# Two fused convolution layers in a software pipeline: folded value weights, three convolution banks, halved transfers and orders written out over all images

## The reference

```python
def _forward(x, gate_w, gate_b, value_w, geom_w, geom_b, pw_w, pw_b):
    gate = einsum('bchw,rc->brhw', x, gate_w) + gate_b ; mu = softmax(gate over r)      # R = 4
    v = einsum('bchw,dc->bdhw', x, value_w)                                             # 1x1, 32 -> 32
    patches = the nine 3x3 neighbours of v, zero padded
    g = einsum('bchw,gc->bghw', x, geom_w) + geom_b   # theta, base, hyper for each r
    ...
    kern = exp(-(pu / sig_u) ** 2 - (ps / sig_s) ** 2)          # nine weights per pixel and r
    w = mu * kern ; w = w / (sum of w over r and the nine + 1e-06)
    agg = einsum('brsl,bcsl->brcl', w, patches)                 # 4 * 32 channels
    return einsum('bkhw,ok->bohw', agg, pw_w) + pw_b            # 128 -> 32
x = x + _forward(gn(x), ...)
x = x + conv3x3(conv3x3(conv3x3(gn(x), w1), w2), w3)            # 32 -> 64 -> 64 -> 32
```

## Time and profile before

| | us |
|---|---|
| median of three runs | 549.23 |
| the profiled execution, its own time | 549.03 |
| its span, first to last instruction | 547.2 |
| outside the span | 1.83 |
| TensorE busy (modelled) | 483.3 |
| VectorE busy | 419.4 |
| ScalarE busy | 216.3 |
| GpSimd busy | 191.4 |

### The profile page before, as it was taken

The page is one execution under the profiler, slowest core; times in us unless marked ns, Lnnn a source line. Parts: engine busy times, 40 slices in busy tenths (PEclk is TensorE's granted clock), DMA queues, the critical chain, the costliest instruction groups (busy, mean ns, idle before and its releaser), DMA issues.

```text
span 547.2 us, 7160 instructions
## 1 busy us (share of the span) xinstructions
PE 483.3 (88%) x2527; PEld 391.8 (72%) x2527; DVE 419.4 (77%) x553; ACT 216.3 (40%) x408; POOL 191.4 (35%) x95
## 2 busy tenths in 40 slices
PE   2505973789999999999999999999999999998995
PEld 2204752566887788777977797779777987886894
DVE  2598678999898989898989989998989698412211
ACT  1520631265335543643355344644364313340110
...
GB/s 145 42 1 0 5 0 56 98 72 17 46 97 100 40 38 87 93 59 44 69 95 69 47 53 107 65 55 41 100 77 25 36 95 86 22 56 107 70 5 38
DMA packets 40275, 32.23 MB, mean 59 GB/s; under 512 B 26160, under 2 KB 30768, under 8 KB 40240
## 3 DMA queue, kind: packets, MB, share of 16 engines
...
## 4 chain that ended last, share of the span: by engine, by line
PE 64%; DVE 16%; issue 9%; SPq 4%; ACT 2%; POOL 1%; DMA 1%; DVEq 0%; ACTq 0%; POOLq 0%
PE conv_ps L366 42%; PE agg_ps L427 7%; DVE prod L712 6%; DVE prod L722 5%; PE val_ps L412 5%; SPq L287 4%; PE geo_ps L395 3%; PE geo_ps L386 3%; PE pw_ps L440 2%; PE conv_ps L380 2%; DMA xraw<-in_x 1%; POOL prod L1003 1%; DVE st L546 1%; DVE trig L643 1%; POOL vs L1019 1%
## 5 line engine op out<-in xcount | busy, mean ns | idle before, releaser
L712 DVE TENSOR_TENSOR prod<-val_ps,tapw 128x2048 f32<-128x2048 f32 x80 | 181.0, 2284 | 11.6 <-PE val_ps L412 10.2
L366 PE MATMUL conv_ps<-c_hi,wc_hi 128*128 128x448 f32 (+2 forms) x384 | 157.1, 409 | 0.0
L366 PE MATMUL conv_ps<-c_hi,wc_lo 128*128 128x448 f32 (+2 forms) x384 | 144.6, 376 | 0.0
L366 PE MATMUL conv_ps<-c_lo,wc_hi 128*128 128x448 f32 (+2 forms) x384 | 144.1, 375 | 0.0
L1003 POOL TENSOR_TENSOR prod<-prod 128x2048 f32<-128x2048 f32 x23 | 112.5, 4894 | 16.4 <-DVE prod L712 16.4
L1019 POOL TENSOR_TENSOR vs<-vn 128x1024 f32<-128x1024 f32 x32 | 69.6, 2185 | 74.2 <-ACT vn L843 73.4
L722 DVE TENSOR_TENSOR prod<-prod 128x2048 f32<-128x2048 f32 x35 | 88.7, 2533 | 1.0 <-POOL prod L1003 0.5
L366 PEld LDWEIGHTS conv_ps<-c_hi,wc_hi 128*128 128x128 f32 x384 | 72.5, 189 | 21.7 <-issue 8.3
L366 PEld LDWEIGHTS conv_ps<-c_hi,wc_lo 128*128 128x128 f32 x384 | 72.3, 188 | 10.6
L366 PEld LDWEIGHTS conv_ps<-c_lo,wc_hi 128*128 128x128 f32 x384 | 72.7, 189 | 9.7 <-issue 2.4
L929 ACT ACTIVATE c_hi<-conv_ps 128x512 fp32r<-128x512 f32 (+4 forms) x88 | 41.9, 485 | 86.4 <-PE conv_ps L366 86.2
...
## 6 DMA issues: line engine op xcount, KB each, us to landing
xq_hi<-y_hi SPq DMA_DIRECT2D x128, 66.0 KB, 2.0
xq_lo<-y_lo SPq DMA_DIRECT2D x128, 66.0 KB, 2.0
...
x2r<-x SPq DMA_DIRECT2D x128, 32.0 KB, 1.9
...
```

The costliest lines, as they stand in the source:

```text
L366: mm = nc.tensor.matmul(bank[:, 0:conv_cols(n)], weights, lo if part == 1 else hi, start=term == part == 0, stop=final and part == 2)
L712: v.tensor_tensor(dst, val.unsqueeze(2).to_broadcast([P, B, R, C]), wgt.unsqueeze(3).to_broadcast([P, B, R, C]), ALU.mult).then_inc(mult_d ...
```

## The change

1. The value matrix is no longer applied to the image. `fold` multiplies it into the pointwise matrix once (`out_w`), and the taps are taken on the normed image: `v_product` and `v_evict` are gone, `norm1_padded` writes the padded copy `xn`, and `xc` has two buffers.
2. `agg_ps` has one bank instead of two, `conv_ps` three instead of two.
3. The high and the low part of y and of xq stand in one tile each, and one DMA moves both: 16 relayout DMAs an image instead of 32. They all wait for the low part.
4. `body` and `on` are gone: each engine's order is a list over all images. In it `store`, `load_x` and `halo` stand elsewhere among the DMAs, and the convolution lags less and less behind the front.

```diff
+N_AGG, N_CONV = 1, 3
+        y = sb("y", [P, 2, 2, K8, PW])
+        y_hi, y_lo = y[:, 0].bitcast(F32R), y[:, 1]
+        xq = sb("xq", [P, 2, H // 2 + 2, PW], F32R)
+            def by_slots(i, g):
                 if g == 0:
+                    wait(y_lo_done, i + 1)
+                    if i >= 1:
+                        wait(conv_done, N_CHUNK * (i - 1) + 4)
                 for s in range(4):
                     j0 = (2, 1, 1, 0)[s] + K8 * g
+                    sp.dma_start(xq[C * s:C * s + C, :, j0:j0 + K8, :].bitcast(F32),
+                                 y[C * g:C * g + C, :, (s + 1) % 2, :, :]).then_inc(xq_in[g], 16)
...
+                    before = N_CHUNK * j + n - N_CONV
+                    if before >= 0:
+                        pj, pn = divmod(before, N_CHUNK)
+                        if pn < N_SPLIT:
+                            wait_lows(pe, pj, pn + 1)
+                        else:
+                            pe.wait_ge(out_done, 2 * pj + pn - N_SPLIT + 1)
...
+            def fold(i, n):
+                if i > 0:
+                    return
+                if n == 0:
+                    pe.wait_ge(front_consts_in, 16 * N_FRONT_CONSTS)
+                    pe.wait_ge(back_consts_in, 16 * N_BACK_CONSTS)
+                    nc.tensor.transpose(pw_ps[:, 0:P], val_w_sb[:, :], ident_sb[:, :]).then_inc(fold_pe, 1)
+                else:
+                    pe.wait_ge(fold_a, 1)
+                    nc.tensor.matmul(pw_ps[:, P:P + C], val_t[:, :], pw_t_sb[:, :], start=True,
+                                     stop=True).then_inc(fold_pe, 1)
...
-            def v_product(i, h):
-                if h == 0:
-                    pe.wait_ge(ch_v, CH_V * i + 1)
-                else:
-                    pe.wait_ge(vc_out, 2 * i + 1)
-                nc.tensor.matmul(geo_ps[:, :], val_w_sb[:, :], xc[:, h * BANK:(h + 1) * BANK],
-                                 start=True, stop=True).then_inc(v_mm, 1)
...
-                if n >= 2 or i >= 1:
-                    pe.wait_ge(agg_sb, 8 * i + n - 1)
+                if 8 * i + n >= N_AGG:
+                    pe.wait_ge(agg_sb, 8 * i + n + 1 - N_AGG)
...
+            def norm1_padded(i):
                 act.wait_ge(gn1_v, GN_V * i + 8)
                 if i >= 1:
                     act.wait_ge(pairs_done, 4 * i)
+                s.activation(xn[:, 1:1 + QR, 1:1 + W], xraw[:, i % 2, :].rearrange("p (r w) -> p r w", w=W),
+                             ACT.Identity, scale=gn1[:, 3:4], bias=gn1[:, 4:5]).then_inc(xp_done, 1)
```

TensorE's new order up to the first back transpose of image 2, and the end of it:

```diff
+gn1_sums(0, 0)
+gn1_sums(0, 1)
+geometry(0)
+gn1_sums(1, 0)
+values(0, 0)
+values(0, 1)
+gn1_sums(1, 1)
+values(0, 2)
+fold(0, 0)
+fold(0, 1)
+values(0, 3)
+values(0, 4)
+geometry(1)
+values(0, 5)
+transpose_sums(0, 0)
+values(0, 6)
+transpose_sums(0, 1)
+values(0, 7)
+transpose_sums(0, 2)
+transpose_sums(0, 3)
+values(0, 8)
+values(0, 9)
+pointwise(0, 0)
+transpose_sums(0, 4)
+values(1, 0)
+transpose_sums(0, 5)
+values(1, 1)
+transpose_sums(0, 6)
+values(1, 2)
+transpose_sums(0, 7)
+pointwise(0, 1)
+values(1, 3)
+values(1, 4)
+values(1, 5)
+gn2_sums(0, 0)
+values(1, 6)
+gn1_sums(2, 0)
+gn2_sums(0, 1)
+gn1_sums(2, 1)
+values(1, 7)
+transpose_sums(1, 0)
+geometry(2)
+transpose_sums(1, 1)
+values(1, 8)
+values(1, 9)
+transpose_sums(1, 2)
+transpose_sums(1, 3)
+convs(0, 0, 8)
+take_high(0, 0)
+convs(0, 8, 11)
+take_high(0, 1)
+take_high(0, 2)
+convs(0, 11, 12)
+pointwise(1, 0)
+values(2, 0)
+convs(0, 12, 14)
+values(2, 1)
+convs(0, 14, 17)
+transpose_sums(1, 4)
+convs(0, 17, 21)
+take_high(0, 3)
+transpose_sums(1, 5)
+take_high(0, 4)
+convs(0, 21, 23)
+transpose_sums(1, 6)
+convs(0, 23, 24)
+transpose_sums(1, 7)
+convs(0, 24, 26)
+values(2, 2)
+pointwise(1, 1)
+values(2, 3)
+convs(0, 26, 28)
+values(2, 4)
+convs(0, 28, 31)
+take_high(0, 5)
+convs(0, 31, 36)
+values(2, 5)
+values(2, 6)
+gn1_sums(3, 0)
+convs(0, 36, 37)
+take_high(0, 6)
+convs(0, 37, 39)
+gn2_sums(1, 0)
+gn1_sums(3, 1)
+take_high(0, 7)
+gn2_sums(1, 1)
+convs(0, 39, 42)
+transpose_sums(2, 0)
...
+convs(6, 29, 34)
+take_high(6, 5)
+convs(6, 34, 36)
+take_high(6, 6)
+convs(6, 36, 38)
+gn2_sums(7, 0)
+convs(6, 38, 40)
+take_high(6, 7)
+gn2_sums(7, 1)
+convs(6, 40, 49)
+take_high(6, 8)
+convs(6, 49, 60)
+convs(7, 0, 60)
```

VectorE's new order up to the products that this transpose needs:

```diff
+gn1_stats(0)
+gn1_spread(0)
+gn1_scale(0)
+gn1_bias(0)
+tap_weights(0, 0)
+tap_weights(0, 1)
+tap_weights(0, 2)
+tap_weights(0, 3)
+split_weights(0)
+tap_weights(0, 4)
+gn1_stats(1)
+tap_weights(0, 5)
+gn1_spread(1)
+tap_weights(0, 6)
+gn1_scale(1)
+tap_weights(0, 7)
+mult(0, 0)
+gn1_bias(1)
+mult(0, 1)
+mult(0, 2)
+mult(0, 3)
+mult(0, 4)
+tap_weights(1, 0)
+tap_weights(1, 1)
+mult(0, 5)
+tap_weights(1, 2)
+mult(0, 6)
+tap_weights(1, 3)
+mult(0, 7)
+mult(0, 8)
+tap_weights(1, 4)
+mult(0, 9)
+tap_weights(1, 5)
+residual(0, 0)
+tap_weights(1, 6)
+tap_weights(1, 7)
+mult(1, 0)
+mult(1, 1)
+mult(1, 2)
+gn2_stats(0, 0)
+residual(0, 1)
+gn2_stats(0, 1)
+mult(1, 3)
+mult(1, 4)
+gn1_stats(2)
+gn2_spread(0)
+gn1_spread(2)
+gn2_scale(0)
+gn1_scale(2)
+add_products(1, 0, 2)
+gn1_bias(2)
+gn2_bias(0)
+add_products(1, 0, 3)
+mult(1, 5)
+split_low(0)
+mult(1, 6)
+mult(1, 7)
+mult(1, 8)
+mult(1, 9)
+tap_weights(2, 0)
+tap_weights(2, 1)
+add_products(1, 1, 1)
+tap_weights(2, 2)
+tap_weights(2, 3)
+add_products(1, 1, 2)
+tap_weights(2, 4)
+add_products(1, 1, 3)
+tap_weights(2, 5)
+residual(1, 0)
+tap_weights(2, 6)
+tap_weights(2, 7)
+mult(2, 0)
+mult(2, 1)
+mult(2, 2)
+residual(1, 1)
+mult(2, 3)
+gn2_stats(1, 0)
+mult(2, 4)
+gn1_stats(3)
+gn2_stats(1, 1)
+gn1_spread(3)
+add_products(2, 0, 2)
+gn2_spread(1)
+gn1_scale(3)
+add_products(2, 0, 3)
...
```

ScalarE's:

```diff
+norm1_padded(0)
+norm1(0)
+split_weights(0)
+tap_weights(0, 0)
+tap_weights(0, 1)
+tap_weights(0, 2)
+tap_weights(0, 3)
+tap_weights(0, 4)
+tap_weights(0, 5)
+fold(0, 0)
+norm1(1)
+norm1_padded(1)
+tap_weights(1, 0)
+sums_out(0, 0)
+tap_weights(1, 1)
+sums_out(0, 1)
+tap_weights(1, 2)
+fold(0, 1)
+sums_out(0, 2)
+tap_weights(1, 3)
+sums_out(0, 3)
+tap_weights(1, 4)
+tap_weights(1, 5)
+sums_out(0, 4)
+sums_out(0, 5)
+sums_out(0, 6)
+sums_out(0, 7)
+norm1_padded(2)
+norm2(0)
+split_high(0)
+norm1(2)
+sums_out(1, 0)
+sums_out(1, 1)
+sums_out(1, 2)
+sums_out(1, 3)
+tap_weights(2, 0)
+high_part(0, 0)
+low_part(0, 0)
+high_part(0, 1)
+high_part(0, 2)
+tap_weights(2, 1)
+tap_weights(2, 2)
+low_part(0, 1)
+tap_weights(2, 3)
+tap_weights(2, 4)
+high_part(0, 3)
+low_part(0, 2)
+sums_out(1, 4)
+tap_weights(2, 5)
...
```

GpSimd's:

```diff
+gn1_rstd(0)
+pair_sum(0, 0)
+pair_sum(0, 1)
+gn1_rstd(1)
+pair_sum(0, 2)
+pair_sum(0, 3)
+add_products(0, 0, 0)
+pair_sum(1, 0)
+pair_sum(1, 1)
+add_products(0, 1, 0)
+pair_sum(1, 2)
+add_products(1, 0, 0)
+pair_sum(1, 3)
+add_products(1, 0, 1)
+gn2_rstd(0)
+gn1_rstd(2)
+pair_sum(2, 0)
+pair_sum(2, 1)
+add_products(1, 1, 0)
+pair_sum(2, 2)
+pair_sum(2, 3)
+add_products(2, 0, 0)
+add_products(2, 0, 1)
...
```

1177 lines of the change are left out of this document (928 added, 249 removed).

## The result

The changed kernel takes 541.7 us (median of 4 runs, 541.2 to 542.8), the kernel before in the same session 548.8: ratio 0.9874, 95% interval 0.9853 to 0.9894. Shorter, as forecast, and clear of the noise, but by 1.3% and not by 3.8%; a threshold of 2% would call it the same. 541.7 lies just outside the range of 516 to 541. The profiled execution took 541.5 us, its span 539.6.

What follows compares the result with a forecast made beforehand. VectorE's chain was taken to bound the fill and TensorE the steady part: 146.5 + 372.2 + 2.4 = 521.1 us for the last matmul, plus 5.9 and 1.83 outside the span, 528.8, stated as 528.5 us, range 516 to 541.

Steps and rivals of the forecast that it cites:

- The fill: Start of the run, by VectorE's list: image 2's first back transpose at 146.5 us, TensorE waiting for VectorE about 7 us.
- The tail: Last image's convolution: norm, splits and joint transfers take 12.5 us, covered by 14.2 us of TensorE work, 1.7 to spare.
- The removed work: Value products of five images behind the first convolution: 10 x 0.86 = 8.6 us off TensorE, the bound engine.
- the shorter walk: Rival, fill: VectorE's list is shorter than summed, TensorE reaches image 2's back transpose at 139; 520 us, chance 0.15.
- transfers by part: Rival, last image: a joint DMA costs as much as two, adding 9 us; 537 us, chance 0.05.
- the one bank at 0.6 us for each transpose: Rival, behind 146.5 us: single agg_ps bank stops each of 48 back transposes, 29 us in all; 556 us, chance 0.04.
- The lower clock: Rival, fill: TensorE runs at its lower clock, image 0's transposes take 3.5 us; 537 us, chance 0.16.
- the walk: VectorE's instructions in the fill, summed in list order to the adds image 2's first back transpose needs, 146.5 us.
- From there TensorE's sum: From image 2's first back transpose to the last matmul: TensorE's work, 372.2 us, plus 2.4 us of waiting.
- Transfers: 0 in the steady part: Joint DMAs save 9.9 us of SyncE per image, which waits anyway in the steady part: worth 0 there.
- the shared port: Fill: VectorE instructions with two SBUF inputs and GpSimd's take turns; the five adds could make it up to 10 us longer.
- priced them at 0 to 1 us in all: Banks: three convolution banks worth 0; one agg_ps bank costs 1 us in all, within the 2.4 us of waiting.

Runs made afterwards that it cites:

- prod_back: Changed kernel with the two value products put back on TensorE for images 3 to 7, their result unread: 549.6 us, 1.0007 of the kernel before.
- old_late: old_order with one more wait, GpSimd's first pair sum of an image held until VectorE's part 3 of its tap weights: 536.4 us, 0.9772 of the kernel before.
- slot3_first: Changed kernel with the same 16 relayout transfers reordered and counted so a first chunk needs five instead of eight: 538.3 us, 0.9799 of the kernel before.
- new_split: Changed kernel with high and low parts in separate transfers, 32 relayout transfers an image instead of 16: 600.5 us, 1.093 of the kernel before.
- recip_norm: Changed kernel with GpSimd's power for both norms replaced by a reciprocal on VectorE, computing other numbers: 542.6 us, 0.9894 of the kernel before.
- norm2_first: Changed kernel with norm2(i) and split_high(i) ahead of image i+2's first norms on ScalarE, images 2 to 5: 546.7 us, 0.9965 of the kernel before.
- pow_free: Changed kernel with a product moved ahead of a VectorE add during GpSimd's power, norm biases ahead of adds, five images: 562.0 us, 1.0222 of the kernel before.
- the four hybrids: Changed kernel's lists for the fill, then old_late's order, with different changeover points or banks: 541.9, 537.1, 546.1 and 553.8 us.
- hybrid4: hybrid3 with the changed kernel's banks, one for back transposes and three for the convolution: 553.8 us, 1.0084 of the kernel before.
- hybrid3: Changed kernel's lists up to image 2's first back transpose, then old_late's order, two banks each: 546.1 us, 0.9947 of the kernel before.
- old_order: All new operations and joint transfers in the kernel before's five repeating orders, two banks each: 552.8 us, 1.0059 of the kernel before.

## Why the prediction was wrong, by its own steps

**Right.** The fill: `mult(0, 0)` 32.05 (33.1 forecast), `mult(1, 0)` 70.53 (68.7), `mult(2, 0)` 127.65 (126), the back transpose of image 2 at 147.86 (146.5), with VectorE as what it waits for. The first convolution came at about 106, not at 102.5: some of the waiting that I had put behind it lay ahead of it. The tail: no stop, transfers at 0.64 us each. The removed work: 8.6 us by the rows, 7.9 by `prod_back` (8.6, less 2.1 of waits, plus 3.1 of clock, less 0.9 of a fill that came out shorter, each from its one profile). Of the rivals, the shorter walk, transfers by part and the one bank at 0.6 us for each transpose did not come. The lower clock did in part: PEclk was 0.50 from 60.2 to 67.0 us, where it had been 1.00, and image 0's fifth back transpose took 3.17 us; from 90 to 106 us it was 0.55 (0.50 before). With the 4.60 us of the tap-weight instruction, which the walk had at under 0.5, this is part of why `mult(1, 0)` came 1.8 us late although `mult(0, 0)` came 1.1 us early. All of it is inside the 1.4 us at the back transpose of image 2, so that term came out partly by errors that cancel.

**Wrong.** One step: "From there TensorE's sum", and in it the waiting, 2.4 us forecast and 13.6 measured. With 1.4 us from the fill that is the whole miss of 12.6 us in the span. The sentence that failed is "VectorE's 52.2 us an image are now less than TensorE's share ... so it runs ahead and its wait goes": I took waiting to be a matter of the share of each engine, and asked only for VectorE. Its adds cost TensorE 0.6 us in one image; xq cost 5.05, ScalarE's parts and VectorE's result 5.4. What made them late is the orders as a whole, since the same operations under the old orders wait little (`old_late`, below). That an image's norm, transfers and low parts now stand where their consumer comes first is my reading of the lists, shown for the transfers alone. What the runs say of it:

- xq: all 5.05 us of xq waits went when the first chunk waited for five transfers instead of eight (`slot3_first`), but only 3.4 us came back in the time, and the same edit is worth nothing in `old_late`. Waits for c_lo grew from 2.4 to 4.5 us, and behind one of them the granted clock was 0.50 from 403.2 to 406.6 us, which costs 1.6. "Transfers: 0 in the steady part" was the same mistake; `new_split` shows that this path has no slack there.
- It is no single instruction. The slow power (`recip_norm`), ScalarE's order (`norm2_first`) and VectorE's (`pow_free`) were each tried, and gained nothing or lost 5 to 20 us. Each list is written to fit the others. (The 1.5 us that `recip_norm` gained behind the fill bound what the power cost, as far as one profile tells.)
- It is not that TensorE cannot be kept full with this work. `old_late`, with all the new operations, waits about 1 us an image; its 55.2 us compare with 55.9 - 1.72 = 54.2 us of work by the earlier trace rows. It gives 536.4 although its convolution begins over 5 us later than the changed kernel's. The remainder to my 528.5 is mostly that start, by this estimate from the rows.

The forecast sum was thus a sum of two things that no kernel here has together, the new fill and a full steady part. Whether they can be had together stays open: the four hybrids lost at the seam what the fill had gained, for reasons of their own, and `hybrid4` lost more behind it. One bank against two was not tried alone in the changed kernel, whose orders need three banks for the convolution. The nearest is `hybrid4` against `hybrid3`: 57.5 us an image against 55.3 to 56.1, so the banks, with the places that they ask for, can cost up to 2 us an image. I had priced them at 0 to 1 us in all; what they cost in the changed kernel's own orders stays open.

**What I had seen and not used.** The prediction weighed the shared port ("SBUF: two separate sides" in the page "SBUF — State Buffer" of the Trainium skill) for the adds of the fill and for two tap-weight instructions of image 0. The trace agrees with it where I did not look: 4.60 us against 0.28 in the changed kernel's own fill, as long as GpSimd's add beside it (4.57); 2.12 us against 0.42 in `old_order`, five times in a row on the path; and the power of one element, 2.53 us beside an add against 0.55:

```profile
145.49 2.53 POOL L1888 TENSOR_TENSOR gn<-gn 128x1 f32<-128x1 f32 x1 [3.52 <-DVE gn L964]
```

Whether such a clash costs anything is a matter of place: the one on VectorE between two awaited adds cost up to 16 us in the run, the one on GpSimd about 1.5 us at the most.
